# SwiGLU mixtures: where VectorE's expert-choice operations stand in a round, and where GpSimd splits the mixture weights

## The reference

```python
x = x + _L0_conv_ref(_ln_c(x), ...)   # linear attention with a batch norm
t = t + _L0_ffn_ref(_ln_t(t), ...)    # SwiGLU, 16 experts, hidden 128
x = x + _L1_conv_ref(...)             # 3x3, kernels mixed per image
t = t + _L1_ffn_ref(...)              # GELU, 8 experts, hidden 256
x = x + _L2_conv_ref(...)             # dynamic 5x5 and dilated 3x3, depthwise
t = t + _L2_ffn_ref(...)              # GELU, 8 experts, hidden 256
x = x + _L3_conv_ref(...)             # deformable 3x3, group norm
t = t + _L3_ffn_ref(...)              # SwiGLU, 16 experts, hidden 128
```

```python
logits = jnp.einsum('bsd,de->bse', x, gate_w) + gate_b
probs = jax.nn.softmax(logits, axis=-1)
top_probs, top_idx = jax.lax.top_k(probs, 2)
top_probs = top_probs / jnp.sum(top_probs, axis=-1, keepdims=True)
dispatch = jnp.sum(jax.nn.one_hot(top_idx, n_experts) * top_probs[..., None], axis=-2)
h1 = jnp.einsum('bsd,edh->bseh', x, w1)
h2 = jnp.einsum('bsd,edh->bseh', x, w2)
hidden = jax.nn.silu(h1) * h2
expert_out = jnp.einsum('bseh,eho->bseo', hidden, w3)
return jnp.einsum('bseo,bse->bso', expert_out, dispatch)
```

## Time and profile before

| | us |
|---|---|
| median of 3 runs (2027.6 to 2030.18) | 2027.83 |
| the profiled execution's own time | 2030.35 |
| its span, first to last instruction | 2028.0 |
| PE busy | 1765.2 (87%) |
| DVE busy | 1169.7 (58%) |
| ACT busy | 987.8 (49%) |
| POOL busy | 852.4 (42%) |
| L552, VectorE's multiplies, 256 times | 244.7 |
| L559, VectorE's gatings, 256 times | 173.2 |
| L597, GpSimd's additions, 256 times | 331.8 |
| L590, GpSimd's half multiplies, 128 times | 165.4 |

### The profile page before, as it was taken

How to read it: one execution, slowest core, us unless ns; L and a number is a source line. 1 busy time by engine, 2 the same in 40 slices (tenths; PEclk the granted TensorE clock), 3 DMA queues, 4 the chain that set the end, 5 groups by cost and what they waited for, 6 DMA issues and landing times. The chain is left out here.

```text
span 2028.0 us, 30736 instructions
## 1 busy us (share of the span) xinstructions
PE 1765.2 (87%) x11371; PEld 977.8 (48%) x11371; DVE 1169.7 (58%) x1559; ACT 987.8 (49%) x1422; POOL 852.4 (42%) x748
## 2 busy tenths in 40 slices
PE   5678999998598999917899988799999948999998
PEld 2534545554244444303444435567776724545454
DVE  5677677766825332395433242655555567777765
ACT  3334545454115666522566641566666634445454
POOL 0146767775104333351333321312112035767677
PEclk8889999999798999956899998899999978999999
DMA  4004333334002222300222240000000003333333
GB/s 109 0 2 106 106 97 106 97 110 139 0 0 58 81 76 73 88 0 0 64 84 76 82 104 1 1 2 2 1 1 1 2 2 85 107 101 108 106 116 98
DMA packets 71580, 121.37 MB, mean 60 GB/s; under 512 B 16962, under 2 KB 18690, under 8 KB 70786
## 3 DMA queue, kind: packets, MB, share of 16 engines
q1 hardware_dynamic: 71426, 119.34, 20.3%
HBM read 115.62 MB, written 3.67 MB: 59 GB/s over the span
## 5 line engine op out<-in xcount | busy, mean ns | idle before, releaser
L597 POOL TENSOR_TENSOR x<-x,mx_gated 128x512 f32<-128x512 f32 x256 | 331.8, 1296 | 142.9 <-DVE mx_gated L559 142.3
L552 DVE TENSOR_TENSOR mx_hidden<-mx_second,mx_hidden 128x1024 f32<-128x1024 f32 (+1 forms) x256 | 244.7, 956 | 196.2 <-PE mx_second L433 194.7
L694 ACT ACTIVATE mx_hidden<-mx_first,w_bias 128x1024 f32<-128x1024 f32 x256 | 264.6, 1114 | 127.0 <-PE mx_first L433 126.8
L734 POOL TENSOR_TENSOR x<-x,mx_gated 128x512 f32<-128x512 f32 x128 | 164.8, 1288 | 285.4 <-DVE mx_gated L711 285.4
L711 DVE SCALAR_TENSOR_TENSOR mx_gated<-mx_out,w_bias,mx_gates 128x512 f32<-128x512 f32 x128 | 96.0, 750 | 287.3 <-PE mx_out L668 265.5
L536 ACT ACTIVATE mx_hidden<-mx_first 128x1024 f32<-128x1024 f32 x256 | 248.9, 1023 | 19.3 <-PE mx_first L433 5.9
L1613 DVE TENSOR_TENSOR c_near_weights<-c_near_hats 128x768 f32<-128x768 f32 x192 | 177.7, 966 | 133.4 <-PE c_near_turned L1493 133.4
L500 PE MATMUL mx_out<-mx_hidden,w_second 128*64 128x512 f32 x1024 | 249.5, 607 | 2.3 <-issue 2.3
L668 PE MATMUL mx_out<-mx_hidden,w_second 128*64 128x512 f32 x1024 | 233.4, 599 | 0.0
L433 PE MATMUL mx_first<-tokens_high,first_high 64*128 64x512 f32 x1024 | 218.9, 423 | 3.0 <-PEq L59 2.9
L528 ACT COPY mx_kept<-mx_second 128x512 f32<-128x512 f32 x128 | 75.2, 587 | 288.2 <-PE mx_second L433 288.2
(11 more groups left out here) (221 smaller groups left out, 2391.7 us busy)
## 6 DMA issues: line engine op xcount, KB each, us to landing
mx_gates<-gate_board SPq DMA_DIRECT2D x768, 128.0 KB, 3.0
w_first<-in_f_first SPq DMA_DIRECT2D x4, 1024.0 KB, 12.0
c_weight<-in_c_weight SPq DMA_DIRECT2D x1, 2304.0 KB
x<-in_x SPq DMA_DIRECT2D x8, 256.0 KB, 4.6
w_second<-in_f_second SPq DMA_DIRECT2D x4, 512.0 KB, 13.1
w_first<-in_f_first SPq DMA_DIRECT2D x4, 512.0 KB, 9.7
out_x<-x SPq DMA_DIRECT2D x16, 128.0 KB, 2.4
gate_board<-xn SPq DMA_DIRECT2D x16, 64.0 KB, 2.5
```

Of the source, the lines that this page charges most:

```text
L552: dve.tensor_tensor(own, second[:, 0:halves, :], own, ALU.mult).then_inc(s.hidden.semaphore, 1)
L597: pool.tensor_tensor(place, place, gated[:, n % GATED, :], ALU.add).then_inc(s.added.semaphore, 1)
L694: act.activation(hidden[:, n % HIDDEN, f], first[:, (n * F + f) % BLOCKS], ACT.Gelu, bias=w.bias1[:, e * F + f:e * F + f + 1]).then_inc(s. ...
L734: pool.tensor_tensor(place, place, gated[:, n % GATED, :], ALU.add).then_inc(s.added.semaphore, 1)
```

## The change

There are three parts.

**Choice operations in the SwiGLU mixtures.** They move from the end of a round to the place between the two multiplies, mostly one a round: 0 and 1 in round 1, 2 and 3 in round 2, 4 to 9 one each in rounds 3 to 8, 10 and 11 in round 9, 12 to 14 in round 11, 15 in round 12, 16 in round 13. In step with that `TURN_AT` goes from 3 to 9, `SQUASH_AT` from 13 to 17, and the post of the rows from step 8 of a chunk to step 13.

**First pair's choice.** In the normalization before each of the four mixtures, operations 0 to 11 of the first pair come after the logits of all four pairs.

**Weights' split.** The whole split (rounding and subtraction, now in pieces of 512 columns) is done by GpSimd in the convolution before the mixture: in the first after its four subtractions (L858), in the second after VectorE has mixed all four kernels (L1128), in the third after its additions (L1223), in the fourth after its memsets (L1351). The high and low parts now live as long as the program, and the loaded weights only as long as the convolution. VectorE has no part of the split any more.

```diff
@@ layer_norm, GpSimd
-                pool.wait_ge(w.loaded, w.all)
                 for i in range(CHUNKS):
-                    pool.tensor_copy(w.high[:, pieces[i]], w.first[:, pieces[i]]).then_inc(g.w_high, 1)
-                for i in range(CHUNKS):
-                    if i < CHUNKS // 2:
-                        pool.wait_ge(g.w_high, split_base + i + 1)
-                        pool.tensor_tensor(w.low[:, pieces[i]], w.first[:, pieces[i]],
-                                           w.high[:, pieces[i]].bitcast(F32), ALU.subtract)
                     pool.wait_ge(g.high, split_base + i + 1)
@@ layer_norm, VectorE
-                staggered((0, centres), (0, split), (4, logits), (1, scales), (2, norm), (5, pick))
+                staggered((0, centres), (4, logits), (1, scales), (2, norm))
+                for j in range(12):
+                    top_two.op(dve, 0, j)
@@ new
+def split_weights(k, pool):
+    w, size = k.w, k.w.high.shape[1]
+    pieces = [slice(i, i + CHUNK) for i in range(0, size, CHUNK)]
+    pool.wait_ge(w.loaded, w.all)
+    for own in pieces:
+        pool.tensor_copy(w.high[:, own], w.first[:, own]).then_inc(k.gt.w_high, 1)
+    for own in pieces:
+        w.split += 1
+        pool.wait_ge(k.gt.w_high, w.split)
+        pool.tensor_tensor(w.low[:, own], w.first[:, own], w.high[:, own].bitcast(F32), ALU.subtract)
@@ Gates.serve, SyncE
-            if e == E // 2 and i + 1 < CHUNKS:
+            if e == post_at and i + 1 < CHUNKS:
@@ mixture_swiglu
-    TURN_AT, SQUASH_AT = 3, 13
+    TURN_AT, SQUASH_AT = 9, 17
...
+        def choose(pair, at):
+            if at < 2:
+                top_two.op(dve, pair, 2 * at)
+                top_two.op(dve, pair, 2 * at + 1)
+            elif at <= 8:
+                top_two.op(dve, pair, at + 2)
+                if at == 8:
+                    top_two.op(dve, pair, 11)
+            elif at == 10:
+                for j in (12, 13, 14):
+                    top_two.op(dve, pair, j)
+            elif at in (11, 12):
+                top_two.op(dve, pair, at + 4)
+
         for n in range(0, STEPS, 2):
             if n >= 2:
                 multiply(n - 1)
+            if n // (2 * E) + 1 < top_two.PAIRS:
+                choose(n // (2 * E) + 1, n % (2 * E) // 2)
             multiply(n)
             if n >= 2:
                 gate(n - 2)
                 gate(n - 1)
-            pair, at = n // (2 * E) + 1, n % (2 * E) // 2
-            ...
-        gates.serve(sp, last_layer)
+        gates.serve(sp, last_layer, TURN_AT + 4)
@@ conv2, GpSimd, after its additions (the same call in conv0, conv1 and offsets)
+            split_weights(k, pool)
```

More of the change, by code:

```diff
@@ L76, in layer_norm @@
             split_base = k.mixtures * CHUNKS
-            size = w.first.shape[1]
-            pieces = [slice(i * size // CHUNKS, (i + 1) * size // CHUNKS) for i in range(CHUNKS)]
         block = ctx.enter_context(nc.Block())
@@ L737, in _ @@
     def _(sp):
-        gates.serve(sp, last_layer)
+        gates.serve(sp, last_layer, E // 2)
     gates.count()
@@ L1060, in _ @@
             pool.memset(kernel[:], 0.0).then_inc(s.cleared, 1)
+            pool.wait_ge(s.kernel, IMAGES)
+            split_weights(k, pool)
         @block.scalar
@@ L1293, in conv3 @@
         off_b, gn_gamma, gn_beta = (cols[:, i:i + 1] for i in range(3))
-        start_at_one(k, k.c3_rest.all)
-        layer_norm(k, turn, 1e-6, loads)
         coords = sb("coords", [P, TILES, 4 * TAPS])
         flag = sb("flag", [1, 2], mybir.dt.int32)
-        offsets(k, PAD, HALF, w_off, off_b, coords, flag)
+        start_at_one(k, k.c3_rest.all)
+        with ExitStack() as early:
+            loads += mixture_loads(k, layer, early)
+            layer_norm(k, turn, 1e-6, loads)
+            offsets(k, PAD, HALF, w_off, off_b, coords, flag)
         y = sb("y", [P, N])
@@ L1940, in mixture_loads @@
     E = m.experts
-    w.first = w.first_room[:, 0:2 * P * E]
+    w.first = ctx.enter_context(k.nc.sbuf_tensor(f"w_first{layer}", [P, 2 * P * E], F32))
+    w.high, w.low = (room[:, 0:2 * P * E] for room in w.parts)
     w.router = w.router_room[:]
@@ L1963, in ffn @@
         tokens = split("tokens", N)
-        w.high, w.low = split("first", 2 * P * m.experts)
         top_two = TopTwo(k, ctx, m)
@@ L2184, in build @@
         k.w = Weights()
-        k.w.first_room = sb("w_first", [P, 2 * P * SWIGLU.experts])
+        k.w.parts = [sb(f"w_{part}", [P, 2 * P * SWIGLU.experts], F32R) for part in ("high", "low")]
+        k.w.split = 0
         k.w.second = sb("w_second", [P, C * SWIGLU.experts])
```

30 lines of the change are left out of this document (7 added, 23 removed).

## The result

The changed kernel takes 1996.43 us (median of 4 runs, 1995.44 to 1997.22), the kernel before 2028.32 in the same series: ratio 0.9841, 95% interval 0.9824 to 0.9858. The forecast was 2002.5, in a range of 1993 to 2013. The profiled execution took 1996.23 with a span of 1994.3, so 33.7 us of span are gone where the sum said 25.6.

The account below looks back on a forecast made before the run. TensorE bounds the mixtures, delayed where choice operations push back VectorE's multiplies. Mixtures -28.8 and -2.2, normalizations -2.0, third convolution +7.4 sum to -25.6 us; from the median 2027.83, forecast 2002.5, range 1993 to 2013.

Parts of the forecast that it names:

- the case that had chance 0.50: SwiGLU gap: VectorE first in some rounds, GpSimd in others; the forecast itself, own range 1997 to 2008 us.
- rival 1: SwiGLU gap: VectorE always goes first, costing 1.2 us a pair; 1998.6 us, chance 0.22.
- rival 2: Third convolution pays nothing because the engines alternate in VectorE's pauses: 7.4 us better, 1994.8 us, chance 0.08.
- What the choice cost: SwiGLU mixtures: choice operations cost 6.6 us a pair, 39.5 us over six pairs, the most their move can give.
- Who is first in the gap: Between the two multiplies: 2.4 us a pair if GpSimd starts first, 1.2 if VectorE does; middle 1.8 taken.
- The slack of 0.42: SwiGLU rounds: the 1024-column multiply may be 0.42 us late free; beyond that the round is as late.
- Rival 3: SwiGLU rounds have no slack, so each pays its full lateness, 4.4 us a pair: 2017.8 us, chance 0.10.
- Start of a mixture: Short multiply follows the gating at once: 1.1 us saved per SwiGLU mixture, 2.2 in all, 0 if gates' DMA rules.
- Turn and post: SwiGLU mixtures: later turn and post of rows cost 0; if the post were late, up to 12 us in all.
- Normalization: Before mixtures: choice after all logits a draw; 1.0 us saved per SwiGLU normalization, 0 for GELU, 2.0 in all.
- Third convolution: GpSimd's split shuts VectorE's tap operations out for each instruction's length, costing 7.4 us.
- Rival 4: SwiGLU gap: GpSimd keeps its turn over both back-to-back instructions, 10 us a pair: 23.6 us slower, 2051, chance 0.05.

Follow-up runs that it names:

- number 9: Changed kernel with third layer's split moved into the normalization before the third convolution, and operations 12 to 16 one a round: 1987.61 us, ratio 0.9789.
- number 11: Changed kernel with VectorE's choice operations held by a signal and three waited-for empty instructions until GpSimd has started its half multiply: 2005.08 us.
- number 6: Changed kernel with useless probe operations of several sizes added to the gap in each SwiGLU mixture's last pair: 2016.55 us.
- number 2: Changed kernel with the first pair's twelve choice operations put back among the normalizations' logits: 1996.64 us, ratio 0.9827.
- number 5: Changed kernel with VectorE's choice operations waiting for a signal from an empty instruction just ahead of GpSimd's half multiply: 1997.86 us, ratio 0.9836.
- number 1: Kernel before with only the new places of the choice operations in the SwiGLU mixtures: 1994.43 us, ratio 0.9819.

## Why the prediction was right, and where its sizes were off

- **The time.** 1996.43 us lies in the stated range, but 6 us below the forecast and just outside the 1997 to 2008 of the case that had chance 0.50. It also lies between rival 1 (1998.6) and rival 2 (1994.8), so the time alone doesn't tell them apart; the traces do, since VectorE was first and the taps did lengthen. (The chances of a faster kernel add up to 0.90, not 0.91.)
- **What the choice cost, and its new place.** Right: 6.6 us a pair before. Now 80.14 - 79.1 = 1.04 remain, and 0.1 in number 9.
- **Who is first in the gap.** This is the term that was mis-sized. I took 1.8 us a pair "since no row decides", the middle between GpSimd first (2.4) and VectorE first (1.2). Both ends were good: 2.25 with GpSimd first (number 11), 1.04 with VectorE first. What happened is rival 1, to which I had given 0.22. VectorE's operation starts when its short multiply is through, 0.05 to 0.06 before GpSimd's. With 33.0 us over six pairs at 5.50 instead of 28.8, this is 4.2 of the 8.1 us that the sum was short.
- **The slack of 0.42.** Right: 0.39 to 0.42 in number 6, but none in the round that holds the turn. Rival 3 is out.
- **Start of a mixture.** Forecast 2.2, measured 1.1. From its first product to its sixteenth long multiply the first mixture took 231.01 - 145.01 = 86.00 us and now takes 224.02 - 143.57 = 80.45: 5.55 less, of which 5.50 are a pair's. The fourth layer's took 86.13 and takes 79.63, 6.50 less. So one start gave next to nothing and the other 1.0. The gatings of both now wait longer for the gates' DMA (1.84 us instead of 0.86, and 1.45 instead of none), which goes the way of the case that I had priced at 0. Why the two starts differ stays open.
- **One stretch of low clock.** Of the 35.7 us, 33.0 are six pairs and 1.1 the starts. Most of the rest is the last pair but one of the fourth layer's mixture before, which took 87.10 us instead of 85.6. The clock stood at 0.50 for 3.41 us in it (the row below, in the view of the clock), just after TensorE had waited 1.89 us for a short multiply at 1905.13. The changed kernel's mixtures have no such stretch within their pairs. It is one event in one profiled execution; how often it comes isn't known, and my sum had no term for it.

```profile
1906.77:1910.18 3.41, 3.41 (x12) 0.50 0.12 41
```

- **Turn and post.** Nothing, as forecast: from 170 us to the end of the first mixture no gating waits for its DMA. The split beside the first and the second convolution costs nothing either: they take 74.95 and 77.55 us, 75.28 and 77.57 before.
- **Normalization.** The 2.0 us came as 2.4. I called the overlap a draw; it is a loss of 0.5 each, and the split's departure gives 1.6 to 1.7 (number 2).
- **Third convolution.** The second term that was mis-sized, 7.4 taken and 4.4 measured: 3.0 of the 8.1. The step said that each GpSimd instruction shuts VectorE out for its length. It does so for all but 0.36 (subtraction) and 0.39 us (rounding of 512 columns). The first additions had shown it already: they cost VectorE 16.5 / 8 = 2.06 us each at 1024 columns (1.96 by the taps' pitch, 3.28 - 1.32), where two additions of 512 take 2.5. I had both numbers and didn't set one against the other.
- **What I had at nothing.** The normalization before the third convolution is 1.84 longer, 1.62 of it by the clock; two other stages are 0.9 shorter each, where the clock rises 3.0 and 2.1 us earlier in the stage. All three are read from the clock's rows, and I have no experiment that moves them by intent. That they cancel to 0.03 us is luck.
- **The 8.1 us that the sum was short**, put together: 4.2 from who is first, 3.0 from the third convolution, 0.4 from the normalizations, 1.6 from the stretch of low clock and what pairs differ, less 1.1 at the starts.
- **Rival 4, slower.** Refused even where GpSimd does come first: VectorE got in after one instruction, not two (number 11).

## What to carry to other kernels

Put small operations of VectorE into the gap where it waits for TensorE, one in each round and before GpSimd's turn. Here the first cost nothing up to 512 columns with two inputs (1024 cost 0.30 us, through GpSimd), and each further one waited for one of GpSimd's instructions unless it was a reduction. Measure how late the critical instruction may be before the next engine notices (0.42 us here), since below that even a lost race is free. Keep GpSimd's two-operand work away from a chain of two-operand VectorE instructions; where it must stand there, cut it into small pieces, and look first for an earlier stage in which GpSimd idles.

## What the runs showed of the hardware that was not expected

- The price of sharing falls with the size of the pieces: the same split cost VectorE's chain 4.4 us in pieces of 512 columns and 5.2 in 1024. In 256 it cost 2.1, or 2.9 had all of it stood beside the chain. Roundings of 256 columns cost it 0.02 us each.
- A lead of 0.01 us decides who waits (number 5). Where VectorE loses, its operation of 256 columns ends 0.27 to 0.29 us after GpSimd's instruction.
- TensorE's clock stood at 0.50 for the first 3 us of the normalization before the third convolution in the changed kernel and in the others that split the weights in the convolutions, and at 1.00 in the kernel before and in number 1, after the same idle time of 2.49 us. What decides it stays open; nothing here was built to tell.
